# Three score banks and three filler banks in a post-norm attention layer, with fillers and PV visits placed anew

## The chip, the cores and the metric

The kernel runs on one core of a Trainium2 chip. The metric is the time of one launch in microseconds, as the device counts it; the median of several runs is given. One more execution was taken by the hardware profiler, and all rows below come from it.

## What is computed

One transformer layer with post-norm, in fp32: B = 4 sequences of S = 1024 tokens, D = 128, H = 16 heads of K = 64, and a feed-forward part with 512 hidden units whose weights are the product of butterfly stages.

```python
q, k, v = (einsum('BSE,EHK->BSHK', x, w) for w in (w_q, w_k, w_v))
logits = einsum('BSHK,BMHK->BSHM', q, k) / sqrt(64)      # causal mask added
a = einsum('BSHM,BMHK->BSHK', softmax(logits + mask), v)
x = layernorm(x + einsum('BSHK,EHK->BSE', a, w_o))
h = gelu(butterfly(x @ W_exp + b_exp, up_weights) + up_bias)
x = layernorm(x + butterfly(h, down_weights) @ W_con + b_con + down_bias)
```

## The kernel before

The attention is cut into 32 **units** (`UNITS`): one pair of heads of one sequence. A unit has 12 **steps** (`STEPS`, line 47): the queries are taken in two chunks of 512 columns, and step (qc, kt) is the tile of 128 keys kt against chunk qc. Chunk 0 has steps 0 to 3, chunk 1 steps 4 to 11. Steps 0 to 3 and 8 to 11 lie on the diagonal; there the columns are 512, 384, 256 and 128, elsewhere 512.

In each step TensorE makes the scores of both heads, two matmuls each (lines 666 and 670), ScalarE takes the exponential out of the bank (line 836), GpSimd masks the diagonal (line 478) and adds up the probabilities (lines 493 to 502), and later TensorE multiplies by V (line 691, called PV here: four matmul instructions a step, the two heads side by side in halves of the array). The scores of head h in step s use score bank (2s + h) mod `NSC`; `exp_done` guards the bank. PV of several steps is done in one **visit**. `PV_AFTER` says after which step's scores which PV steps come; negative ones are steps of the unit before (-5 is step 7, -1 is step 11).

Between all that stand **fillers**, the work for the next unit, each of which writes one of `NWORK` work banks in turn and has to wait until the filler that had the bank before is drained (`take_work`, line 573 on):
- `proj` (lines 592 to 594): q or k of the next unit for one chunk. ScalarE copies the high part (line 773), VectorE subtracts it for the low part (line 885). `proj (0, 0)` is made one unit earlier than the others.
- `v` (602 to 604): V for two tiles and two units, drained by ScalarE.
- `max` (616): scores of the next unit once more, of which VectorE takes the row maximum (lines 960, 963). `MAXES` has 21 of them.
- `mt` (621): the transposed maxima; VectorE casts them (973), and a DMA puts them into row K of QL (line 390), for which the second score matmul of the next unit waits (`m_landed`).
- `norm` (653): sums of the probabilities of the unit before, by ones, in 32-column parts of the array. ScalarE copies them out (823). Then come DMA RCOL (395), VectorE's reciprocal (1024), DMA RROW (398), two broadcasting DMAs R (401), and `scale` on VectorE (1030), which frees the PV banks O. The first PV step of each chunk waits for it (`o_free`).
- `out` (631), `lay` (624), `x1` (636), `w2` (640): output projection and preparations of the feed-forward part.

`FILL[s]` has three lists of fillers for step s: BETWEEN the scores of its two heads, BEHIND them, and LATE, behind the PV visit. Every engine walks the same order: TensorE in `window` (line 695 on), ScalarE in its loop over steps, VectorE in its own `window`. VectorE does `recip` after the fillers of step `RECIP_AFTER` and `scale` after those of `SCALE_AFTER`. GpSimd composes the butterfly weights in steps `COMPOSE_AFTER`. The PSUM banks are two for scores (SC), two for O and four WORK, eight in all.

After the last unit the feed-forward part runs on TensorE (`up`, line 741, and `down`, line 753), with four hidden banks and two y banks out of SC and WORK.

Of the kernel before, what the change touches and what calls it, by code (L numbers as in the profile page):

```python
# [72 lines left out]

PV_AFTER = {1: [-5, -4, -3, -2, -1], 8: [0, 1, 2, 3], 9: [4, 5, 6]}
PV_LEFT = [s + NS for ss in PV_AFTER.values() for s in ss if s < 0]
# [10 lines left out]
FILL = [[[], [], []] for _ in range(NS)]  # L86
FILL[0] = [[], [], [("proj", 1, 0)]]
FILL[1] = [[], [("proj", 0, 1), ("proj", 1, 1)], [("norm", 1)] + MAXES[0:1]]
FILL[2] = [[], [("v", 0)], MAXES[1:2]]
FILL[3] = [MAXES[2:3], MAXES[3:5], []]  # L90
FILL[4] = [[], [("v", 1)] + MAXES[5:6], []]
FILL[5] = [MAXES[6:7], [], MAXES[7:9]]
FILL[6] = [[], [], MAXES[9:11]]
FILL[7] = [MAXES[11:13], [], MAXES[13:14]]
FILL[8] = [MAXES[14:15], [], MAXES[15:17]]
FILL[9] = [MAXES[17:18], MAXES[18:21], []]
FILL[10] = [[("mt",)], [("proj", 0, 0)], []]
COMPOSE_AFTER = [4, 5, 9]
RECIP_AFTER = 2
SCALE_AFTER = 6  # L100
OUT_AT = ((11, 1), (11, 2))
FILLERS = [(s, place, f) for s in range(NS) for place in range(3) for f in FILL[s][place]]
# [9 lines left out]
assert all(len(ops) == 1 for ops in COMPOSE.values()) and max(unit for unit, _ in COMPOSE) < UNITS  # L112
NWORK = 4
LAY_UNITS = TILES // 2
# [51 lines left out]

NSC = 2
assert 2 * NS % NSC == 0 and LAST_PROJ in PREFETCH

# [19 lines left out]
def post_norm_layer(nc, x, w_q, w_k, w_v, w_o, W_exp, b_exp, up_w, up_b, down_w, W_con, b_con, down_b, out):  # L189
    ctx = ExitStack()  # L190
    with ctx:
# [105 lines left out]
        def lays_after(n):  # L297
# [4 lines left out]
        lay_banks = [SC[0][:, :], SC[1][:, :], O[0][:, :], O[1][:, :]]  # L302
        hid_banks = [SC[0][:, :], SC[1][:, :], WORK[(LAST_NORM - 1) % NWORK][:, :],
                     WORK[LAST_NORM % NWORK][:, :]]
        y_banks = [WORK[LAST_OUT % NWORK], WORK[(LAST_OUT + 1) % NWORK]]

# [244 lines left out]
        def _(pe):  # L551
# [182 lines left out]
            def up(g):  # L734
                pe.wait_ge(x1t_copied, g + 1)
                for t_ in range(HT):
                    if g == 0 and t_ >= 2:
                        evacuated(LAST_NORM - 3 + t_)
                    if g > 0:
                        pe.wait_ge(gelu_done, (g - 1) * HT + t_ + 1)  # L740
                    nc.tensor.matmul(hid_banks[t_], W1[:, t_ * P:(t_ + 1) * P], x1T[g % EARLY_GROUPS], start=True,  # L741
                                     stop=True).then_inc(hid_ready, 1)
# [393 lines left out]
```

## Time and profile before

| what | us |
|---|---|
| runs: median (lowest to highest) of 3 | 1051.42 (1051.22 to 1052.35) |
| the profiled execution | 1050.42 |
| its span, first to last instruction | 1048.5 |
| busy: TensorE matmuls | 1014.8 (97%) |
| busy: VectorE | 753.1 (72%) |
| busy: GpSimd | 757.2 (72%) |
| busy: ScalarE | 602.8 (57%) |
| mean granted TensorE clock | 0.989 |

The profile calls the engines PE (TensorE matmuls), PEld (its weight loads), DVE (VectorE), ACT (ScalarE), POOL (GpSimd) and SP. A matmul's time in the timeline runs from its start to its modelled end and overlaps the next one's; what it costs the sequence is seen in the distance of the starts.

### The profile page before, as it was taken

How to read it: one execution, taken by the hardware profiler on the slowest of the kernel's cores; microseconds unless marked ns; L12 is line 12 of the kernel's file. 1: busy time of each engine (PE TensorE's matmuls, PEld its weight loads, DVE VectorE, ACT ScalarE, POOL GpSimd, SP SyncE). 2: the span in 40 equal slices, each digit the busy share in tenths (PEclk: the TensorE clock that was granted, in tenths of full speed). 3: DMA queues.
4: the chain of work that ended last, by engine and by line, in shares of the span. 5: the costliest groups of instructions: out<-in, count | busy, mean ns of one | idle time of the engine just before them, and what ended most of it. 6: DMA issues, size and time to landing. Idle time of an engine off the chain costs nothing.

```text
span 1048.5 us, 17665 instructions
## 1 busy us (share of the span) xinstructions
PE 1014.8 (97%) x5816; PEld 697.7 (67%) x5816; DVE 753.1 (72%) x2013; ACT 602.8 (57%) x1214; POOL 757.2 (72%) x725
## 2 busy tenths in 40 slices
PE   4799999999999999999999999999999999999997
PEld 3556667676667766767666766676666676665576
DVE  6666777677677777776778777877777778773446
ACT  4355566665566565666666656666555655664431
POOL 6278877777779777777778877777777887777322
PEclk9699999999999999999999999999999999999999
DMA  7112223223131223232232222332313212220002
GB/s 222 44 45 67 59 58 82 63 82 79 45 81 42 73 52 83 62 82 62 64 80 55 63 58 53 82 82 63 81 43 81 68 47 72 62 62 22 22 19 63
DMA packets 45800, 68.69 MB, mean 66 GB/s; under 512 B 15079, under 2 KB 21515, under 8 KB 45710
## 3 DMA queue, kind: packets, MB, share of 16 engines
q1 hardware_dynamic: 45710, 67.57, 25.2%
q8 instruction: 47, 0.77, 0.3%
q14 instruction: 43, 0.35, 0.1%
HBM read 31.11 MB, written 2.36 MB: 32 GB/s over the span
## 4 chain that ended last, share of the span: by engine, by line
PE 91%; DMA 3%; DVE 2%; POOL 2%; issue 1%; SPq 1%; ACT 0%; POOLq 0%; DVEq 0%; ACTq 0%
PE O L691 25%; PE WORK L616 14%; PE SC L666 13%; PE SC L670 12%; PE WORK L631 5%; PE WORK L653 3%; PE WORK L753 3%; PE WORK L594 3%; PE WORK L592 3%; PE WORK L593 3%; PE WORK L602 1%; PE WORK L604 1%; PE WORK L603 1%; PE SC L741 1%; PE WORK L741 1%; DMA R<-RROW 1%
## 5 line engine op out<-in xcount | busy, mean ns | idle before, releaser
L836 ACT ACTIVATE PR<-SC 128x512 f32<-128x512 f32 (+3 forms) x768 | 354.9, 490 | 278.2 <-PE SC L670 251.9
L493 POOL TENSOR_TENSOR SUM<-SUM,PR 128x1024 f32<-128x1024 f32 (+3 forms) x256 | 418.9, 1636 | 14.9 <-POOL SUM L502 0.5
L960 DVE CUSTOM_DVE_ANT_0 WORK<-WORK,CMASK 128x128 f32<-128x128 f32 (+3 forms) x512 | 239.1, 513 | 65.9 <-PE WORK L616 65.8
L666 PE MATMUL SC<-QH,KHL 128*128 128x512 f32 (+3 forms) x768 | 271.9, 359 | 4.8 <-ACT PR L836 3.2
L670 PE MATMUL SC<-QL,KH 128*128 128x512 f32 (+3 forms) x768 | 262.8, 346 | 0.0
L478 POOL TENSOR_SCALAR_AFFINE_SELECT PR<-PR 128x256 f32<-128x256 f32 x256 | 105.8, 415 | 206.1 <-ACT PR L836 205.9
L616 PE MATMUL WORK<-KHL,QH 128*128 128x512 f32 (+3 forms) x768 | 225.1, 361 | 5.4 <-DMA KH<-KHL 4.0
L691 PE MATMUL O<-PR,VLO 128*64 128x512 f32 (+3 forms) x1024 | 200.0, 522 | 1.2 <-DVE OT L1030 1.0
L666 PEld LDWEIGHTS SC<-QH,KHL 128*128 128x128 f32 x768 | 145.2, 189 | 63.8 <-ACT PR L836 29.2
L616 PEld LDWEIGHTS WORK<-KHL,QH 128*128 128x128 f32 x768 | 135.8, 191 | 56.0 <-issue 35.3
L963 DVE TENSOR_REDUCE MP<-WORK 128x1 f32<-128x512 f32 x256 | 164.2, 683 | 4.7
L670 PEld LDWEIGHTS SC<-QL,KH 128*128 128x128 f32 x768 | 145.5, 189 | 10.3
L885 DVE TENSOR_TENSOR QL<-WORK,QH 64x512 fp32r<-64x512 f32 x128 | 88.0, 688 | 78.8 <-ACT QH L773 77.6
L502 POOL TENSOR_TENSOR SUM<-PR 128x768 f32<-128x768 f32 x64 | 136.6, 2134 | 1.4 <-ACT PR L836 1.4
L691 PEld LDWEIGHTS O<-PR,VLO 128*64 128x64 f32 x1024 | 64.9, 136 | 105.6 <-issue 77.6
L885 DVE TENSOR_TENSOR KHL<-WORK,KHL 64x512 fp32r<-64x512 f32 x128 | 88.1, 689 | 38.3 <-ACT KHL L773 36.2
L773 ACT ACTIVATE QH<-WORK 64x512 fp32r<-64x512 f32 x128 | 75.6, 590 | 27.8 <-PE WORK L594 27.0
L773 ACT ACTIVATE KHL<-WORK 64x512 fp32r<-64x512 f32 x128 | 75.8, 593 | 4.7 <-PE WORK L594 1.4
L691 PE MATMUL O<-PR,VHI 128*64 128x256 f32 (+3 forms) x512 | 74.3, 432 | 0.0
L960 DVE DVE_READ_ACCUMULATOR2_ANT MP<- 128x1 f32 x512 | 72.1, 141 | 0.0
L691 PEld LDWEIGHTS O<-PR,VHI 128*64 128x64 f32 x512 | 36.8, 137 | 52.6 <-issue 46.0
L631 PE MATMUL WORK<-WOT,OT 128*128 128x128 f32 x512 | 63.7, 278 | 0.0
(100 smaller groups left out, 1070.5 us busy)
## 6 DMA issues: line engine op xcount, KB each, us to landing
QH<-QH SPq DMA_DIRECT2D x128, 128.0 KB, 2.3
KH<-KHL SPq DMA_DIRECT2D x128, 128.0 KB, 2.3
R<-RROW SPq DMA_DIRECT2D x64, 256.0 KB, 3.9
SW<-in_L_ffn_up_weights_dram SPq DMA_DIRECT2D x9, 512.0 KB, 4.6
SW<-_L_ffn_down_weights_dram SPq DMA_DIRECT2D x9, 512.0 KB, 4.4
out_dram<-X SPq DMA_DIRECT2D x8, 256.0 KB, 2.3
X<-in_L_attn_x_BSE_dram SPq DMA_DIRECT2D x1, 512.0 KB, 4.6
WQKV<-in_L_attn_w_q_dram SPq DMA_DIRECT2D x1, 512.0 KB, 5.4
```

The lines of the kernel that those rows point to most:

```text
L493: nc.gpsimd.tensor_tensor(total, total, prob(unit, s), ALU.add).then_inc(add_done, 1)
L502: nc.gpsimd.tensor_tensor(total, first[:, :, START[s]:], prob(unit, s), ALU.add).then_inc(add_done, 1)
L616: t = nc.tensor.matmul(w[:, at_col:at_col + n], QH[:, nxt, h, qt * P:(qt + 1) * P], KHL[:, nxt, h, lo:lo + n], start=True, stop=True)
L631: t = nc.tensor.matmul(w[:, k * P:(k + 1) * P], attended(pair, qc)[:, k * P:(k + 1) * P], WOT[:, pair % PAIRS, :], start=pair < last, stop ...
L666: nc.tensor.matmul(dst, KHL[:, par, h, kt * P:(kt + 1) * P], QH[:, par, h, q0:q0 + n], start=True, stop=False)
L670: nc.tensor.matmul(dst, KH1[:, par, h, kt * P:(kt + 1) * P], QL[:, par, h, q0:q0 + n], start=False, stop=True).then_inc(scores_ready, 1)
L691: t = nc.tensor.matmul(O[qc][h * K:(h + 1) * K, START[s]:], values(unit, kt)[:, h * K:(h + 1) * K], p[:, h, :], start=kt == 0, stop=s == L ...
L773: return nc.scalar.activation(dst, src, ACT.Copy)
L836: nc.scalar.activation(prob(unit, s)[:, h, :], SC[use % NSC][:, 0:n], ACT.Exp, scale=K ** -0.5).then_inc(exp_done, 1)
L885: return nc.vector.tensor_tensor(dst, src, hi_part.bitcast(F32), ALU.subtract)
L960: op = nc.vector.tensor_tensor_reduce(cols, cols, CMASK[:, CH - n:], 1.0, LOWEST, ALU.add, ALU.max, cell)
L963: op = nc.vector.tensor_reduce(cell, cols, AX_X, ALU.max)
```

## The change

The score banks become three, the work banks three; with the two O banks it is eight as before. The PV visits stand after steps 0, 2, 8 and 10 in place of 1, 8 and 9. The fillers are placed anew: three projections together in step 0, norm in step 2 ahead of the PV visit there, both v fillers in step 3, `mt` and `proj (0, 0)` behind the visit of step 10, and one of the output fillers with them. `scale` comes one step later, a compose step stands in step 0 in place of 4. The hidden banks of the feed-forward part are the three score banks and one work bank.

```diff
-PV_AFTER = {1: [-5, -4, -3, -2, -1], 8: [0, 1, 2, 3], 9: [4, 5, 6]}
+PV_AFTER = {0: [-5, -4, -3], 2: [-2, -1], 8: [0, 1, 2, 3], 10: [4, 5, 6]}
...
-FILL[0] = [[], [], [("proj", 1, 0)]]
-FILL[1] = [[], [("proj", 0, 1), ("proj", 1, 1)], [("norm", 1)] + MAXES[0:1]]
-FILL[2] = [[], [("v", 0)], MAXES[1:2]]
-FILL[3] = [MAXES[2:3], MAXES[3:5], []]
-FILL[4] = [[], [("v", 1)] + MAXES[5:6], []]
-FILL[5] = [MAXES[6:7], [], MAXES[7:9]]
-FILL[6] = [[], [], MAXES[9:11]]
-FILL[7] = [MAXES[11:13], [], MAXES[13:14]]
-FILL[8] = [MAXES[14:15], [], MAXES[15:17]]
-FILL[9] = [MAXES[17:18], MAXES[18:21], []]
-FILL[10] = [[("mt",)], [("proj", 0, 0)], []]
-COMPOSE_AFTER = [4, 5, 9]
+FILL[0] = [[("proj", 1, 0), ("proj", 0, 1), ("proj", 1, 1)], [], []]
+FILL[1] = [MAXES[0:1], MAXES[1:2], MAXES[2:3]]
+FILL[2] = [[], [("norm", 1)], MAXES[3:5]]
+FILL[3] = [[("v", 0), ("v", 1)] + MAXES[5:6], [], MAXES[6:7]]
+FILL[4] = [[], MAXES[7:8], []]
+FILL[5] = [[], [], MAXES[8:9]]
+FILL[6] = [MAXES[9:10], [], MAXES[10:11]]
+FILL[7] = [MAXES[11:12], [], MAXES[12:13]]
+FILL[8] = [MAXES[13:14], MAXES[14:16], MAXES[16:18]]
+FILL[9] = [[], MAXES[18:19], MAXES[19:20]]
+FILL[10] = [MAXES[20:21], [], [("mt",), ("proj", 0, 0)]]
+COMPOSE_AFTER = [0, 5, 9]
 RECIP_AFTER = 2
-SCALE_AFTER = 6
-OUT_AT = ((11, 1), (11, 2))
+SCALE_AFTER = 7
+OUT_AT = ((10, 2), (11, 1))
...
-NWORK = 4
+NWORK = 3
...
-NSC = 2
+NSC = 3
...
-        hid_banks = [SC[0][:, :], SC[1][:, :], WORK[(LAST_NORM - 1) % NWORK][:, :],
-                     WORK[LAST_NORM % NWORK][:, :]]
+        hid_banks = [SC[0][:, :], SC[1][:, :], SC[2][:, :], WORK[LAST_NORM % NWORK][:, :]]
...
-                    if g == 0 and t_ >= 2:
-                        evacuated(LAST_NORM - 3 + t_)
+                    if g == 0 and t_ == NSC:
+                        evacuated(LAST_NORM)
```

## Rows read from the trace of the kernel before

**Rows 1.** The page: engine busy time; the granted clock in 40 slices, in tenths

```profile
PE 1014.8 (97%) x5816; PEld 697.7 (67%) x5816; DVE 753.1 (72%) x2013; ACT 602.8 (57%) x1214; POOL 757.2 (72%) x725
PEclk9699999999999999999999999999999999999999
```

**Rows 2.** TensorE's waits at score banks (us, times, longest): 79 to 920 us; whole span

```profile
PE SC L666 <- ACT PR L836: 1.2, 1, 1.2
...
PE SC L666 <- ACT PR L836: 3.2, 6, 1.2
```

**Rows 3.** Timeline of TensorE, 506 to 519 us (start, us, engine, line)

```profile
506.90 0.27 PE L621 MATMUL WORK<-IDN,NEGM 128*128 128x128 f32 x1
...
510.40 0.39 PE L670 MATMUL SC<-QL,KH 128*128 128x512 f32 x1
...
511.56 0.40 PE L594 MATMUL WORK<-XTL,WST 128*128 128x512 f32 x1
...
513.64 0.39 PE L594 MATMUL WORK<-XTL,WST 128*128 128x512 f32 x1
513.96 1.08 PE L691 MATMUL O<-PR,VLO 128*64 128x512 f32 x4
...
517.12 1.06 PE L653 MATMUL WORK<-SUM,ONES 128*32 128x512 f32 x8
518.12 0.50 PE L616 MATMUL WORK<-KHL,QH 128*128 128x128 f32 x2
```

**Rows 4.** Timeline of TensorE, 524 to 537 us

```profile
524.86 0.42 PE L666 MATMUL SC<-QH,KHL 128*128 128x512 f32 x1
525.12 0.39 PE L670 MATMUL SC<-QL,KH 128*128 128x512 f32 x1
...
528.50 2.37 PE L691 MATMUL O<-PR,VLO 128*64 128x512 f32 x16
...
533.20 2.79 PE L691 MATMUL O<-PR,VLO 128*64 128x512 f32 x12
535.93 0.38 PE L666 MATMUL SC<-QH,KHL 128*128 128x256 f32 x1
536.15 0.28 PE L670 MATMUL SC<-QL,KH 128*128 128x256 f32 x1
```

**Rows 5.** Timeline of TensorE's weight loads, 513 to 515 us

```profile
513.19 0.19 PEld L593 LDWEIGHTS WORK<-XTH,WST 128*128 128x128 f32 x1
513.42 0.19 PEld L594 LDWEIGHTS WORK<-XTL,WST 128*128 128x128 f32 x1
513.96 0.20 PEld L691 LDWEIGHTS O<-PR,VLO 128*64 128x64 f32 x4 [0.35 <-ACT PR L836]
514.44 0.14 PEld L691 LDWEIGHTS O<-PR,VHI 128*64 128x64 f32 x2 [0.29 <-issue]
514.87 0.14 PEld L691 LDWEIGHTS O<-PR,VHI 128*64 128x64 f32 x2 [0.28 <-issue]
```

**Rows 6.** Score matmuls of 512 columns by form: busy us, mean ns, idle before

```profile
L666 PE MATMUL SC<-QH,KHL 128*128 128x512 f32 x384 | 158.8, 413 | 4.5 <-ACT PR L836 3.0 <-issue 1.5
...
L670 PE MATMUL SC<-QL,KH 128*128 128x512 f32 x384 | 151.4, 394 | 0.0
```

**Rows 7.** Timeline of ScalarE: one projection's two copies

```profile
511.99 1.20 ACT L773 ACTIVATE KHL<-WORK 64x512 fp32r<-64x512 f32 x2
```

**Rows 8.** Timeline of VectorE: one projection's subtractions; scale

```profile
515.19 1.39 DVE L885 TENSOR_TENSOR QL<-WORK,QH 64x512 fp32r<-64x512 f32 x2 [0.58 <-ACT QH L773]
...
527.54 1.29 DVE L1030 TENSOR_TENSOR OT<-O,R 128x512 f32<-128x512 f32 x2 [0.47 <-DMA R<-RROW]
```

**Rows 9.** VectorE's waits for R, whole span (us, times, longest)

```profile
DVE OT L1030 <- DMA R<-RROW: 15.2, 17, 6.0
```

**Rows 10.** Timeline of SyncE's DMA queue: issue of the row of maxima

```profile
507.51 0.55 SPq L390 DMA_DIRECT2D QL<-NROW  x1
```

**Rows 11.** DMA issues, 506 to 512 us: KB each, median us to landing

```profile
QL<-NROW SPq DMA_DIRECT2D x1, 8.0 KB, 1.8
```

## The prediction

> **What bounds the kernel now.** I read the page's engine shares first, then TensorE's waits, then its timeline, then the engines that feed it. The page has TensorE at 1014.8 of 1048.5 us, and the granted clock at nine tenths or more of 2.4 GHz in all but the second of 40 slices [rows 1]. A busy TensorE may still lose time inside matmuls that start late, so the share alone decides nothing. Two further views do. In the 841 us of the loop between the first and the last units, TensorE waits once for anything, 1.2 us at a score bank [rows 2]. And in the timeline its matmuls start one behind the other: a matmul of 512 columns takes 0.23 us from its start to the next one's (the loads for L593 and L594 in [rows 5] are 0.23 apart). So TensorE's own sequence sets the time, and an edit is worth what it adds to or takes from that sequence, plus any wait it makes or removes.
>
> What is in the sequence beyond the columns? The PV matmuls use the array in halves (128*64, two heads beside each other), everything else in the loop but norm uses all of it. The timeline in [rows 3] shows the way in: L594 at 513.64 would be followed at 513.87, but the first L691 starts at 513.96, **0.09 us late**. The weight loads in [rows 5] show why: within a run of one kind the weights are loaded ahead (those of the L594 that starts at 513.64 at 513.42), while the first PV weights load only at 513.96, with the matmul itself. Inside the run the loads come 0.43 us apart for a pair of heads, but the first pair takes 0.48 (513.96 to 514.44): **0.05 more**. The way out: the visit at 533.20 has six pairs, 6 x 0.43 = 2.58, plus the 0.05, and the next matmul would start at 535.83; it starts at 535.93, **0.10 late**, and the 256-column matmul behind it takes 0.22 instead of 0.12, **0.10 more** [rows 4]. One separate visit therefore costs 0.09 + 0.05 + 0.10 + 0.10 = **0.34 us** besides its work, by what shows at its ends, whatever it holds: the visit and norm from 513.96 to 518.12 come, with ten pairs and norm's two sets of four, to 3.01 + 0.86 of columns in 4.16, which leaves 0.29 for the inside of two modes [rows 3].
>
> **The change part by part.** *PV visits.* Before there are three blocks a unit: after step 1 (five PV steps, norm right behind them), after 8, after 9. After the change there are four: after 0 (three steps), after 2 (two steps, norm right ahead of them), after 8, after 10. The columns are the same; one block more is new. The previous unit's two visits stand in units 1 to 31: 31 x 0.34 = **+10.5 us**, all on TensorE's sequence, so all on the path. Norm in front of PV in place of behind costs nothing more: the block goes into one mode, over to the other and out of it either way, and norm keeps its 1.00 us (517.12 to 518.12) [rows 3].
>
> The Trainium skill, TensorEngine Tiling (Array Packing), section Key Properties, says that a change of tiling mode drains TensorE. This trace agrees with the drain and gives it the price of 0.34 us for in and out. By that rule the change as a whole is bought with one more drain a unit; it is the rule that speaks against it.
>
> *Third score bank.* What can it give? Score matmuls of line 666 (the ones that wait for a bank) average 413 ns at 512 columns, those of 670, which never do, 394: 19 ns x 384 = 7.3 us is the most that can hide there [rows 6]; part of it is the way out of other modes. In a unit's timeline the late starts at score banks are of the kind of 524.86 to 525.12, 0.26 in place of 0.23 [rows 4], at two or three places of the unit: nearer to 0.055 x 31 = 1.7 us. I take **-1.7** and keep -7.3 as the bound. It does more where few fillers stand between scores, in the first two units and the last: over the whole span the visible waits for a score bank are 3.2 us in 6 places [rows 2]. In the last unit the visit after step 8 waits for R behind them, so not all comes back; I take **-2.0** for all edges, between 0 and -4.
>
> *Three filler banks.* A filler waits for the drain of the third before it, not the fourth. The tight place is the start of the unit: three projections stand together in step 0. Reckoned from its first score: two score matmuls 0.47, the first projection's third matmul at 0.94, and ScalarE starts 0.43 us after such a start (511.99 against 511.56), so at 1.37 [rows 3, 7]. ScalarE needs 1.20 for each projection [rows 7]: the first is handed on at 2.57. VectorE needs 1.39 each and a little between them [rows 8], three in a row: 6.8. TensorE comes to the filler that needs the third projection's bank after 0.47 + 2.08 (projections) + 0.47 + 0.09 + 2.51 (PV) + 0.10 + 0.35 + 0.23 + 0.35 + 0.23 = 6.88 (narrower ones by columns from the 0.23 of 512; PV of 1408 columns as two times two pairs of 0.43 and two of 0.32, and 0.15 of the mode). Spare 0.1, which the semaphores nearly take. Norm comes at 7.63. The others, gone through in the same way, have 0.15 us or more. I take 31 x 0.02 = **+0.7**, from 0 to 31 x 0.5 = +15 if VectorE comes late by half a microsecond (see the third rival). The prologue has 29 fillers through three banks, with VectorE as its bound and a DMA wait that absorbs part: **+0.5**, 0 to +1.5.
>
> *Norm later, and the chain behind it.* Norm stands one step later. Behind it: the evacuation, RCOL, recip, RROW, the broadcast R, then scale, whose first half frees O for PV after step 8. In the unit shown scale starts at 527.54, 10.42 us after norm (517.12), and its two halves take 1.29, so the first ends at 11.06 [rows 3, 8]. VectorE waits for R 17 times, 15.2 us in all and 6.0 the longest [rows 9]: some 0.6 us at a time in half of the units, 0.47 in the one shown. So the end moves by about half a microsecond to either side of 11. TensorE reaches the visit 11.38 us after norm today (528.50 minus 517.12) [rows 3, 4]; in the new order the work between is 1.00 norm, 0.80 + 0.10 PV, 0.41 two maxes, 0.44 step 3, 1.43 v, 0.23 + 0.22 maxes, 4 x 0.94 steps 4 to 7 with 0.94 of maxes, step 8 with 0.64, and 0.09 in: 11.2. So only the late units wait, some 0.05 us on average: **+1.5**, 0 to +12.
>
> *mt behind the visit of step 10, proj (0,0) behind it.* mt (506.90) to the second score matmul of the next unit (510.40) is 3.50 us today [rows 3]; in the new order 0.11 + 0.70 + 1.76 + 0.45 + 0.31 = 3.3. What the matmul waits for: the cast and issue at 507.51, 0.61 after mt, plus 1.8 of transfer = 2.4 [rows 10, 11]. No wait in units with an output filler; 0. The moved maxes and compose steps (GpSimd, at 72% busy, is no nearer to the path) and the new bank list of the tail change no sum on TensorE: 0.
>
> Sum: 10.5 - 1.7 - 2.0 + 0.7 + 0.5 + 1.5 = **+9.5 us**. The profiled execution took 1050.42 us (span 1048.5, 1.9 around it); with the sum 1059.9. The median is 1.0 above the profiled one: **1060.9 us**, +0.9%.
>
> **The rivals.** *The new block is hidden or as cheap as nothing* (the change of mode costs only where something else waits too): 1051.4 - 3.7 + 2.7 = **1050.4**, no change. Against it: three visits of different size show the same cost, at places where all inputs had long been there.
>
> *Faster: the score bank hides more than the visit costs.* Place: the score matmuls of steps 4 to 8, where the plan after the change has one or two fillers a step. If all 7.3 us are bank waits and the new visit costs less than 0.14 us, it ends below 1049: 31 x 0.1 - 7.3 - 2.0 + 2.7 = -3.5, **1048**. From 0.14 us a visit on it isn't faster. The measured 0.34 speaks against.
>
> *Bank starvation.* The 0.05 us of the third projection's bank is missed by VectorE, e.g. behind an output sum or a normalise step of the step before: each 0.5 us is 15: **1076**. For it: the spare is nil. Against: VectorE has waits of its own for ScalarE ahead of the first projection.
>
> *The R chain ends last* at the visit after step 8: each 0.35 us more there is +11: **1072**. For it: 0.1 us of spare against a spread of about 1 us.
>
> **How the numbers follow.** Forecast 0.66, block hidden 0.08, faster 0.08, starvation 0.10, R chain 0.08. The forecast's own bounds are 1056 to 1066. Leaving 0.1 out on either side, the range goes to 1053 below (part of the block hidden) and to 1070 above (either wait in part). About 0.2% is what a measurement of this kernel can tell from no change: faster 0.08, same 0.08, slower 0.84.
>
> **What would show it.** Right: TensorE still over 96% busy; visits at steps 0 and 2 each with a late first start (0.09) and a late matmul behind (0.10 + 0.10); a unit some 0.35 us longer; no wait lines for work banks. Starvation would show in TensorE's waits for VectorE's L885 or L960 at line 616 in step 1; the chain as waits of L691 for L1030; a faster kernel as a unit that is not longer though it has four blocks. What would make it wrong: a mode change whose cost depends on its neighbours, or a wait inside today's 'busy' matmuls that I took for the cost of a mode.

## Result: slower by 2.2%, and the profile after

| | before | after |
|---|---|---|
| median of the runs beside each other, us | 1051.87 (4 runs) | 1075.35 (4 runs, 1072.56 to 1077.79) |
| ratio to before, 95% interval | 1 | 1.0223 [1.0197, 1.0249] |
| profiled execution, us | 1050.42 | 1072.56 |
| its span, us | 1048.5 | 1070.6 |
| mean granted clock | 0.989 | 0.988 |

The change costs 23.5 us. The forecast had 9.5 and the range ended at 1070. In the lines quoted from here on, the line numbers of the kernel after are one lower than those of before: the filler that waits at L616 before waits at L615, the scores' L666 and L670 are L665 and L669, PV's L691 is L690, VectorE's L885, L960, L985, L1013 and L1030 are L884, L959, L984, L1012 and L1029, and so on. The kernels with four filler banks keep the numbers of before.

The profile's page of the kernel after: the engines' busy time with its share of the span, and the shares of the chain that ended last. They answer [rows 1]; the line of the granted clock is the same as there. The third line is the chain of the kernel before.

```profile
PE 1028.8 (96%) x5816; PEld 710.6 (66%) x5816; DVE 778.5 (73%) x2013; ACT 611.0 (57%) x1214; POOL 763.4 (71%) x725
PE 82%; DVE 9%; DMA 5%; issue 1%; ACT 1%; POOL 1%; SPq 1%; POOLq 0%; ACTq 0%; DVEq 0%
PE 91%; DMA 3%; DVE 2%; POOL 2%; issue 1%; SPq 1%; ACT 0%; POOLq 0%; DVEq 0%; ACTq 0%
```

TensorE is busy for 1028.8 us in place of 1014.8, with exactly as many matmuls and the same clock; its idle time went from 33.7 to 41.8 us. So 14.0 of the 22.1 us sit inside what the page calls busy, and 8.1 outside. The chain that ended last runs over VectorE for 9% of the span (before: 2%). That is the first sign that not only TensorE's own sequence got longer.

TensorE's waits in the loop, from 79 to 940 us (engine, what it made, line, the engine and line waited for: us in all, how many, the longest). They answer [rows 2], where one wait of 1.2 us stood for the whole loop:

```profile
PE O L690 <- DVE OT L1029: 3.3, 3, 1.4
PE WORK L591 <- DVE X L984: 3.2, 8, 0.6
PE WORK L615 <- DVE KHL L884: 1.7, 4, 0.5
PE SC L669 <- DMA QL<-NROW: 1.1, 2, 0.8
PE WORK L620 <- DVE NEGM L966: 0.9, 1, 0.9
```

With one more of 0.2 these are 10.4 us, and nearly all are waits for VectorE: a PV visit for the scale of O, a projection for the output sum, a max filler for a projection's cast, mt for the last maxes. A view of waits lists only idle time; a matmul that starts late while its forerunner still counts as busy is not in it. So I went through the timeline by distances from start to start. It shows this in the loop: the third projection (of the three that stand together in step 0) late in nine of the units by 0.48 to 0.81 (some 5 us, and 1 us behind it), the maxes of step 1 late by up to 0.70 in six units, and what stands behind the third of them late by 0.1 in some twenty (some 4.5), PV behind step 8 late by 0.96, 1.46 and 1.13 in the first unit of the second, third and fourth sequence (3.5), the row of maxima that the DMA puts into QL late in three of the first four units after unit 0 (2.4), and mt late twice (1.7). Each is measured against the usual distance at its place, so together they need not give the whole.

One such unit on TensorE (start, duration, engine, line, operation, output and inputs, shape, count, and in brackets the idle time ahead with its releaser); it answers [rows 3]:

```profile
579.91 0.39 PE L593 MATMUL WORK<-XTL,WST 128*128 128x512 f32 x1
580.61 0.50 PE L591 MATMUL WORK<-XTH,WST 128*128 128x512 f32 x1 [0.31 <-DVE X L984]
...
586.20 0.45 PE L615 MATMUL WORK<-KHL,QH 128*128 128x384 f32 x1 [0.29 <-DVE KHL L884]
```

And VectorE in the same stretch:

```profile
578.91 0.93 DVE L1012 TENSOR_SCALAR X<-X,MV,RSTD 128x128 f32<-128x128 f32 x1
579.87 0.69 DVE L984 TENSOR_TENSOR X<-WORK,X 128x512 f32<-128x512 f32 x1
...
581.91 1.39 DVE L884 TENSOR_TENSOR KHL<-WORK,KHL 64x512 fp32r<-64x512 f32 x2
...
584.75 1.39 DVE L884 TENSOR_TENSOR KHL<-WORK,KHL 64x512 fp32r<-64x512 f32 x2
586.18 0.30 DVE L959 CUSTOM_DVE_ANT_0 WORK<-WORK,CMASK 128x128 f32<-128x128 f32 x1
```

The third projection (580.61) should start 0.23 us after 579.91, that is at 580.14. Its bank is the one of the output filler, which stands three fillers before it. VectorE frees it with the output sum at 579.87 to 580.56, and that had stood behind a normalise step (578.91) that took 0.93 us: 0.47 us late. The three casts of projections then go back to back until 586.14, and the max at 586.20 has to wait for the last. With four banks, as before, neither waits.

Which units are late follows from VectorE's list. An output sum stands at the start of every unit from unit 3 on. In every second one from unit 12 to unit 30 a normalise stands ahead of it, and nine of these ten are the ones with the late third projection (in the tenth, unit 22, the normalise took 0.36 us). Four statistics of 0.87 us in all and their aggregates, between the sum and the first cast, stand in units 9, 10, 17, 18, 25 and 26. These are the units whose maxes are latest (0.70 in 17 and 25, 0.45 in 18 and 26, 0.37 in 9), but for unit 10 with 0.09.

### The profile page after: what moved, and what is told of

Same layout as the page of the kernel before. It is cut to its first block, busy times and chain, and to the rows that moved or that the text cites. A ratio compares the mean times of both kernels' runs of the same rounds, so it can differ in the third digit from the quotient of the medians.

```text
span 1070.6 us, 17665 instructions
## 1 busy us (share of the span) xinstructions
PE 1028.8 (96%) x5816; PEld 710.6 (66%) x5816; DVE 778.5 (73%) x2013; ACT 611.0 (57%) x1214; POOL 763.4 (71%) x725
## 3 DMA queue, kind: packets, MB, share of 16 engines
HBM read 31.11 MB, written 2.36 MB: 31 GB/s over the span
## 4 chain that ended last, share of the span: by engine, by line
PE 82%; DVE 9%; DMA 5%; issue 1%; ACT 1%; POOL 1%; SPq 1%; POOLq 0%; ACTq 0%; DVEq 0%
PE O L690 23%; PE WORK L615 13%; PE SC L665 11%; PE SC L669 11%; PE WORK L630 3%; PE WORK L652 3%; PE WORK L752 3%; PE WORK L591 2%; DVE QL L884 2%; PE WORK L593 2%; PE WORK L592 2%; PE SC L740 2%; DMA R<-RROW 1%; DVE X L1012 1%; PE WORK L601 1%
## 5 line engine op out<-in xcount | busy, mean ns | idle before, releaser
L492 POOL TENSOR_TENSOR SUM<-SUM,PR 128x1024 f32<-128x1024 f32 (+3 forms) x256 | 419.2, 1638 | 14.6 <-ACT PR L835 0.5
L959 DVE CUSTOM_DVE_ANT_0 WORK<-WORK,CMASK 128x128 f32<-128x128 f32 (+3 forms) x512 | 243.0, 511 | 74.7 <-PE WORK L615 72.0
L477 POOL TENSOR_SCALAR_AFFINE_SELECT PR<-PR 128x256 f32<-128x256 f32 x256 | 108.7, 425 | 222.1 <-ACT PR L835 220.8
L665 PE MATMUL SC<-QH,KHL 128*128 128x512 f32 (+3 forms) x768 | 265.5, 351 | 1.5 <-issue 1.5
L669 PE MATMUL SC<-QL,KH 128*128 128x512 f32 (+3 forms) x768 | 261.8, 345 | 1.9 <-DMA QL<-NROW 1.9
L615 PE MATMUL WORK<-KHL,QH 128*128 128x512 f32 (+3 forms) x768 | 238.6, 363 | 6.2 <-DVE KHL L884 3.3
L690 PE MATMUL O<-PR,VLO 128*64 128x512 f32 (+3 forms) x1024 | 201.6, 526 | 7.0 <-DVE OT L1029 7.0
L962 DVE TENSOR_REDUCE MP<-WORK 128x1 f32<-128x512 f32 x256 | 172.2, 687 | 19.1 <-PE WORK L615 19.1
L665 PEld LDWEIGHTS SC<-QH,KHL 128*128 128x128 f32 x768 | 145.2, 189 | 36.8 <-issue 14.9
L615 PEld LDWEIGHTS WORK<-KHL,QH 128*128 128x128 f32 x768 | 135.8, 190 | 36.9 <-issue 12.3
L669 PEld LDWEIGHTS SC<-QL,KH 128*128 128x128 f32 x768 | 145.2, 189 | 20.2 <-DMA QL<-NROW 2.8
L690 PEld LDWEIGHTS O<-PR,VLO 128*64 128x64 f32 x1024 | 65.5, 137 | 104.4 <-issue 73.8
L884 DVE TENSOR_TENSOR QL<-WORK,QH 64x512 fp32r<-64x512 f32 x128 | 88.0, 688 | 56.5 <-ACT QH L772 54.6
L884 DVE TENSOR_TENSOR KHL<-WORK,KHL 64x512 fp32r<-64x512 f32 x128 | 88.2, 689 | 23.5 <-ACT KHL L772 21.4
L690 PE MATMUL O<-PR,VHI 128*64 128x256 f32 (+3 forms) x512 | 81.2, 439 | 0.0
L690 PEld LDWEIGHTS O<-PR,VHI 128*64 128x64 f32 x512 | 34.0, 136 | 66.8 <-issue 40.3
L959 DVE DVE_READ_ACCUMULATOR2_ANT MP<- 128x1 f32 x512 | 72.1, 141 | 0.0
```

Of the source, the lines that this page charges most:

```text
L477: nc.gpsimd.affine_select(out=tri, in_=tri, compare_op=ALU.is_ge, fill=fill, base=0, pattern=[[0, 2], [1, P]], channel_multiplier=-1).then ...
L492: nc.gpsimd.tensor_tensor(total, total, prob(unit, s), ALU.add).then_inc(add_done, 1)
L615: t = nc.tensor.matmul(w[:, at_col:at_col + n], QH[:, nxt, h, qt * P:(qt + 1) * P], KHL[:, nxt, h, lo:lo + n], start=True, stop=True)
L665: nc.tensor.matmul(dst, KHL[:, par, h, kt * P:(kt + 1) * P], QH[:, par, h, q0:q0 + n], start=True, stop=False)
L669: nc.tensor.matmul(dst, KH1[:, par, h, kt * P:(kt + 1) * P], QL[:, par, h, q0:q0 + n], start=False, stop=True).then_inc(scores_ready, 1)
L690: t = nc.tensor.matmul(O[qc][h * K:(h + 1) * K, START[s]:], values(unit, kt)[:, h * K:(h + 1) * K], p[:, h, :], start=kt == 0, stop=s == L ...
```

## Experiments

All kernels compute the whole layer; only plans and bank counts differ. Times are medians with the range and the number of runs, ratios stand against the kernel before on the same chip (1051.6 to 1051.9). Distances of norm are those of two neighbouring units for which the view of waits lists nothing. The first five take the change apart, the others take its waits apart.

### One block more, on the plan before

```diff
-PV_AFTER = {1: [-5, -4, -3, -2, -1], 8: [0, 1, 2, 3], 9: [4, 5, 6]}
+PV_AFTER = {1: [-5, -4, -3], 2: [-2, -1], 8: [0, 1, 2, 3], 9: [4, 5, 6]}
```

> The kernel before with one edit: PV steps 10 and 11 of the unit before are multiplied after step 2 in place of step 1 (31 more visits). Theory A (a mode change costs 0.34 us wherever it stands): +10.5 us over before, 1062. Theory B (the loss of the change is in one more visit alone): +22 to +24, 1075. Theory C (all of the loss comes from the filler banks, a visit costs nothing of its own): 1051 to 1053.

Measured: 1066.51 us (1064.52 to 1067.57, 4), ratio 1.0137 [1.0122, 1.0152]: +14.6. Norm's start in two neighbouring units, of before and then of this kernel:

```profile
253.82 1.07 PE L653 MATMUL WORK<-SUM,ONES 128*32 128x512 f32 x8
282.97 1.06 PE L653 MATMUL WORK<-SUM,ONES 128*32 128x512 f32 x8
```

```profile
256.58 1.06 PE L653 MATMUL WORK<-SUM,ONES 128*32 128x512 f32 x8
286.08 1.06 PE L653 MATMUL WORK<-SUM,ONES 128*32 128x512 f32 x8
```

29.15 and 29.50 us: the block costs 0.35, 31 of them 10.9. The whole came out 4.5 above the 1062 that I had expected. Beyond the blocks, the profiled execution shows some 3.5 us in the loop, mostly late starts of maxes (up to 0.36) in every second unit, and a last unit with tail that is 2.6 longer. So the block's price is as forecast, and this plan has so little slack that a shift of two PV steps makes some maxes late even with four filler banks.

### The banks alone, on the plan before

```diff
-NWORK = 4
+NWORK = 3
-NSC = 2
+NSC = 3
```

(and the tail's list of banks as in the change)

> The kernel before with three score banks and three filler banks and nothing else replanned. Theory A: the score banks give back up to 2 us; the filler banks cost what VectorE is late by, in the old plan perhaps 0 to 5 us: 1050 to 1056. Theory C (three filler banks starve TensorE in any plan): +15 or more, 1066 and up. Theory D (the third score bank alone is worth something): below 1049.

Measured: 1124.71 us (1123.88 to 1128.28), ratio 1.0704 [1.0683, 1.0725]: **+73**, the largest loss but one of all. I had expected next to nothing of it. TensorE's waits from 79 to 940 us, a late max on TensorE, and VectorE beside it:

```profile
PE WORK L615 <- DVE MP L959: 21.6, 27, 2.2
```

```profile
534.85 0.40 PE L669 MATMUL SC<-QL,KH 128*128 128x512 f32 x1
...
535.87 0.50 PE L615 MATMUL WORK<-KHL,QH 128*128 128x512 f32 x1 [0.63 <-DVE MP L959]
```

```profile
534.14 1.28 DVE L1029 TENSOR_TENSOR OT<-O,R 128x512 f32<-128x512 f32 x2
```

VectorE works its list in order. While it scales O for 1.28 us, it frees no filler bank, and the plan before has its maxes in tight groups around that place. Four banks bridge it, three don't. The list of waits holds only 21.6 of the 73 us; but the order of TensorE's matmuls is that of before, so the starts can be compared one by one: in the loop the maxes start 52 us later in sum, the scores behind them 11. A third score bank gives nothing visible back here. So the change bears three filler banks only because it also regroups the fillers.

### The new plan on the old banks, and on two score banks with three fillers

```diff
-NWORK = 3
+NWORK = 4
-NSC = 3
+NSC = 2
```

> The changed kernel with two score banks and four filler banks as before: the new plan alone. Theory A: the waits for VectorE at filler banks (third projection 6 us, maxes 5 us) go, but with few fillers between the scores of steps 4 to 7 two score banks don't do: a bank comes back 1.42 us after its scores started, and the plan has 1.17 us a step there, 0.25 us in three steps of each unit, 24 us: 1080 to 1090. Rival (the score banks were idle anyway): 1062 to 1065.

Measured: 1100.85 us (1100.28 to 1101.57), ratio 1.0465 [1.0449, 1.048]: 25.5 slower than the kernel after, and 11 above what I had expected at most. The second kernel keeps NWORK at 3 and takes one score bank away (`NSC = 2`).

> The changed kernel with two score banks in the attention, three filler banks (the third score bank is used in the feed-forward part alone): what the third score bank is worth in the new plan. Theory A: +15 to +25 over the changed kernel, 1090 to 1100. Rival (as the forecast had it for the old plan, up to 2 us): 1075 to 1078.

Measured: 1111.53 us (1108.96 to 1111.83), ratio 1.0558 [1.054, 1.0575]: 36 slower than the kernel after, again 11 above the expectation. TensorE in the first of these two kernels, from one start of two score steps and one filler to the next such start, and ScalarE beside it:

```profile
517.17 0.50 PE L666 MATMUL SC<-QH,KHL 128*128 128x512 f32 x1
...
518.21 0.40 PE L616 MATMUL WORK<-KHL,QH 128*128 128x512 f32 x1
518.59 0.50 PE L666 MATMUL SC<-QH,KHL 128*128 128x512 f32 x1
```

```profile
516.51 1.09 ACT L836 ACTIVATE PR<-SC 128x512 f32<-128x512 f32 x2 [0.38 <-PE SC L670]
517.94 1.09 ACT L836 ACTIVATE PR<-SC 128x512 f32<-128x512 f32 x2 [0.34 <-PE SC L670]
```

Between the two starts TensorE has five matmuls of 512 columns, 5 x 0.23 = 1.15 us, and takes 1.42 for them. That is a bank's own round: ScalarE's two exponentials take 1.09, and then it has to wait 0.34 until TensorE has filled the banks again, while TensorE has waited for ScalarE. The plan of the change runs steps this close together and holds its fillers in bulk elsewhere; there the third score bank is worth 36 us. The plan before seldom meets that round (one listed wait at a score bank in the loop, [rows 2]). So the bank and the plan belong together in both directions: new banks on the old plan +73, new plan on the old banks +49, both together +23.5.

These two kernels have the same plan and the same two score banks in the attention, so they also price the fourth filler bank on the new plan: 1111.53 - 1100.85 = **10.7 us**. TensorE's waits at filler banks from 79 to 940 us, first with four filler banks, then with three (the waits for mt left out of the second list are the same 1.4):

```profile
PE WORK L621 <- DVE NEGM L967: 1.4, 2, 0.7
```

```profile
PE WORK L591 <- DVE X L984: 3.2, 9, 0.6
PE WORK L615 <- DVE KHL L884: 0.9, 4, 0.3
```

With four banks there is no wait of a projection for the output sum and none of a max for a cast; with three both are there. By starts, projections are 6.3 us later in the loop and maxes 2.0. The waits for mt are there with four banks too.

### Two visits in place of three, on the plan before

```diff
-PV_AFTER = {1: [-5, -4, -3, -2, -1], 8: [0, 1, 2, 3], 9: [4, 5, 6]}
+PV_AFTER = {1: [-5, -4, -3, -2, -1], 8: [0, 1, 2, 3, 4, 5, 6]}
```

> The kernel before with PV steps 4 to 6 moved from the visit after step 9 into the one after step 8: one block of PV less in each of 32 units. Theory A (a mode change costs 0.34 to 0.36 us wherever it stands, VectorE has slack in the old plan with four filler banks): 32 x 0.35 = 11 us less, 1041. Rival (VectorE is so near to the bound that 5 us of TensorE without a max leave it idle, and the maxes behind it wait): 1048 to 1056.

Measured: 1126.19 us (1124.27 to 1127.08), ratio 1.0703 [1.0687, 1.0719]. A block less and yet +74, where I had expected -11. Its waits:

```profile
PE WORK L621 <- DVE NEGM L967: 63.7, 32, 2.3
```

The visit behind step 9 was cover: while TensorE does PV there, VectorE ends the last maxes that mt needs. Without it TensorE waits some 2 us for them in each of the 32 units. A visit can't be taken away for 0.34 us if it hides somebody; this is what made me look for a pair of visits whose joining hides nobody.

### The normalise step moved to step 5

The rival of the starvation named a normalise step or an output sum ahead of the projections' casts. This kernel takes the normalise away from there.

```diff
-NORMALISE_AT = {t: ((t // TILES + 1) * PAIRS + 3 + t % TILES, 10) ...
-NORMALISE_AT |= {t: ((B - 1) * PAIRS + 3 + t % TILES // 2, 9 + t % 2) ...
+NORMALISE_AT = {t: ((t // TILES + 1) * PAIRS + 3 + t % TILES, 5) ...
+NORMALISE_AT |= {t: ((B - 1) * PAIRS + 3 + t % TILES // 2, 5 + t % 2) ...
```

> The changed kernel, with each normalise step of VectorE moved from step 10 (9 and 10 in the last sequence) to step 5 (5 and 6). Theory A: the 10 waits of the third projection for the output sum (0.5 to 0.8 us each, 6 us with what follows them) go, and a part of the waits at the third and fourth max: 1066 to 1070. Theory B (only the visit counts): 1075 as it is.

Measured: 1080.40 us (1078.55 to 1081.59), ratio 1.027 [1.0255, 1.0285]: 5 slower, not 7 faster. The third projection's waits are gone, so the normalise was their cause; but the maxes behind its new place wait:

```profile
PE WORK L615 <- DVE MP L962: 5.4, 6, 1.3
```

In steps 5 and 6 the gap between fillers is too short for the step, which takes 0.48 to 2.36 us there. A miss of the number, and a hint that the step is dearer than the 0.35 us of its best case.

### The same, to step 9

```diff
-NORMALISE_AT = {t: ((t // TILES + 1) * PAIRS + 3 + t % TILES, 10) ...
+NORMALISE_AT = {t: ((t // TILES + 1) * PAIRS + 3 + t % TILES, 9) ...
```

> The changed kernel with the normalise step of VectorE one step earlier (9 in place of 10) for the first two sequences: into the place before mt where VectorE stands idle 1.6 us a unit in the changed kernel. Theory A (the third projection waits for the bank of the output sum because normalise stands ahead of it): seven or eight of the ten waits there go, 4 to 5 us less and nothing new in their place: 1070 to 1071. Rival (as when it was moved to step 5, any place behind which VectorE has maxes to do costs more than it saves): 1076 or more.

Measured: 1075.95 us (1074.21 to 1076.78), ratio 1.0226 [1.0212, 1.024]: no change to the kernel after, where I had expected 5 us less. Waits of TensorE over the whole span:

```profile
PE WORK L620 <- DVE NEGM L966: 9.0, 12, 1.4
```

Most of the third projection's waits went, mt's came in their place, and PV waited in five units of the loop in place of three. A short normalise of this kernel, and what GpSimd did beside it:

```profile
392.14 0.35 DVE L1012 TENSOR_SCALAR X<-X,MV,RSTD 128x128 f32<-128x128 f32 x1
```

```profile
391.99 0.42 POOL L477 TENSOR_SCALAR_AFFINE_SELECT PR<-PR 128x256 f32<-128x256 f32 x1
```

### The normalise in the gap behind mt's cast

Before the next unit's first projection, VectorE waits for TensorE and ScalarE. If the normalise is issued right behind the cast of mt, it stands in that wait and ahead of nobody that has its input. The edit puts the loop over NORMALISE_AT behind the consumer of mt, and skips step 10 at its old place (the last unit excepted):

```diff
                             consume(u, f, n)
+                        if f[0] == "mt":
+                            for t, when in NORMALISE_AT.items():
+                                if when == (u, s):
+                                    dve.wait_ge(rstd_made, t // TILES + 1)
+                                    normalise_tile(t, x1_made)
```

> The changed kernel with the same placing of normalise, nothing else. Theory A: the waits of the third projection in the eight units behind a normalise step go (4.6 us) without the waits for scale and at mt that came when it stood at step 9: 1070 to 1071. Rival (the VectorE work only moves): 1075.

Measured: 1068.22 us (1067.46 to 1068.77), ratio 1.0157 [1.0143, 1.0171]: **7.1 us** less than the kernel after, by nothing but the place of the normalise steps in VectorE's list. It fell 2 us below what I had expected. The order of TensorE's matmuls is the same in both, so the starts can be compared: in the loop the projections give back 5.6 us and the maxes 2.2, which the expectation had left out, while other starts come 2.8 later.

### One block less on the new plan, three times

Norm and both of the previous unit's visits go into one block behind step 0:

```diff
-PV_AFTER = {0: [-5, -4, -3], 2: [-2, -1], 8: [0, 1, 2, 3], 10: [4, 5, 6]}
+PV_AFTER = {0: [-5, -4, -3, -2, -1], 8: [0, 1, 2, 3], 10: [4, 5, 6]}
-FILL[0] = [[("proj", 1, 0), ("proj", 0, 1), ("proj", 1, 1)], [], []]
+FILL[0] = [[("proj", 1, 0), ("proj", 0, 1), ("proj", 1, 1)], [], [("norm", 1)]]
-FILL[2] = [[], [("norm", 1)], MAXES[3:5]]
+FILL[2] = [[], [], MAXES[3:5]]
```

> The changed kernel, with all five PV steps of the unit before after step 0 and norm right behind them, so three blocks a unit as before. Theory A: 31 x 0.34 = 10.5 us less, and the waits for scale after step 8 (3.5 us) and at the third max (3.4 us) go, since norm comes 1 us earlier and the maxes 1.7 us later: 1057 to 1062. Theory C (filler banks are all): 1070 to 1075.

Measured: 1077.28 us (1075.73 to 1078.08), ratio 1.024 [1.0225, 1.0255]; a miss by 15 to 20. The block's 0.34 us is saved, and each unit waits at a max bank, 0.36 us on average in the list and up to 0.5:

```profile
PE WORK L615 <- DVE MP L959: 11.3, 31, 0.5
```

The visit and norm in step 2 were the cover behind which VectorE caught up with the maxes. The next kernel draws the five maxes of steps 2 to 4 apart on top of it:

```diff
-FILL[2] = [[], [], MAXES[3:5]]
-FILL[3] = [[("v", 0), ("v", 1)] + MAXES[5:6], [], MAXES[6:7]]
-FILL[4] = [[], MAXES[7:8], []]
+FILL[2] = [[], [], MAXES[3:4]]
+FILL[3] = [[("v", 0), ("v", 1)] + MAXES[4:5], [], MAXES[5:6]]
+FILL[4] = [[], MAXES[6:7], MAXES[7:8]]
```

> The changed kernel with all five PV steps and norm after step 0, and the fifth to ninth max each one place later, so that VectorE has time: Theory A (in the run without that, the 0.34 us of the visit came back and went into a wait of 0.5 us for the bank of the second max before, in every unit): 15 us less than that run, 1062. Rival (VectorE's backlog from the three projections is only moved to the next place): 1070 to 1077.

Measured: 1069.61 us (1068.01 to 1070.73), ratio 1.0166 [1.0151, 1.0181], so 7.7 less, half of the 15 that I had expected; the rest of the wait moved on to v:

```profile
PE WORK L601 <- DVE MP L959: 5.5, 30, 0.3
```

A v filler is drained by another engine than the maxes. So the third of these kernels puts v 0 among them, where it gives VectorE time, and the normalise to step 9:

```diff
+FILL[2] = [[], [], [("v", 0)]]
+FILL[3] = [MAXES[3:4], [("v", 1)], MAXES[4:5]]
+FILL[4] = [MAXES[5:6], MAXES[6:7], MAXES[7:8]]
```

> One block for PV and norm after step 0, the first v filler (which ScalarE drains) moved between the maxes in step 2, the other fillers of steps 3 and 4 spread, normalise in step 9. Theory A (what the change loses is one block of PV a unit and the waits for VectorE, and both can be taken out of it): the 0.34 us a unit wait of the run before goes (10 us) and most waits of the third projection (5 us): 1069.6 - 15 = 1055. Rival (VectorE's backlog appears elsewhere): 1062 or more. Below 1049 would mean that three score banks pay after all.

Measured: 1056.58 us (1055.37 to 1059.02, 5), ratio 1.0049 [1.0037, 1.0062]: as expected. What waits is left in it:

```profile
PE WORK L620 <- DVE NEGM L966: 6.7, 9, 1.4
```

### The block back in, while mt waits

The last kernel with the visit split again (`0: [-5, -4, -3], 2: [-2, -1]`), norm staying in the first block.

> The same with the last two PV steps of the unit before after step 2, so one block of PV more in each of 31 units: the price of a block in the plan with three filler banks. Theory A: +0.36 us x 31 = +11 over the run beside it. Rival (in the new plan a block gives VectorE time, so that part of it is got back): +3 to +7.

Measured: 1075.89 us (1074.56 to 1076.53), ratio 1.023 [1.0214, 1.0245]: 19.3 more, not 11. The undisturbed units are 0.32 longer, which is 10 us; the other 9 are mostly these, 15.2 in place of 6.7:

```profile
PE WORK L620 <- DVE NEGM L966: 15.2, 21, 1.4
```

With the normalise in step 9, mt waits for the last maxes in 21 units in place of 9. Why in more of them was not tried; but I could not use this pair to price the block, hence the next two.

### The cleaned pair: nearly all waits taken away, with and without the block

The kernel with one block and v 0 among the maxes, with the normalise behind mt's cast:

> The one-block plan with v early (1056.6), with the normalise step of VectorE between mt's cast and the next projection, where VectorE waits 1.65 us for ScalarE in every unit, in place of ahead of the last maxes. Theory A (TensorE's waits for the maxima at mt, 0.75 us in six units of the first three sequences, are the 1.1 us of normalise): 6 x 0.75 = 4.5 less, 1052, and perhaps a little under the kernel before. Rival (it isn't normalise, the maxes are late anyway): 1056 to 1057.

Measured: **1050.07 us** (1048.66 to 1052.74, 11 runs) against 1051.69 (15 runs), ratio 0.9984 [0.9974, 0.9993]. It is the best of all kernels here. It is 0.16% below the one before, and the interval ends only just below 1. What TensorE waits for from 79 to 930 us:

```profile
PE SC L669 <- DMA QL<-NROW: 1.3, 2, 0.8
PE WORK L620 <- DVE NEGM L966: 0.7, 1, 0.7
```

Its twin has the visit split again and nothing else changed:

> The first of these three with the last two PV steps after step 2 again: the price of one more block where normalise is out of the way. Theory A (a block costs 0.34 us of mode change and pushes the last maxes nearer to mt only behind normalise): +10 to +12 over the first, 1063. Rival (a block costs what the earlier pair of runs showed, 19 us, because any later place of the maxes makes mt wait): +17 to +20, 1070.

Measured: 1061.13 us (1060.17 to 1061.37), ratio 1.0089 [1.0075, 1.0102]: 11.06 more, as expected, 0.357 for each of 31 blocks. Norm's starts in two neighbouring units, first of the one-block kernel, then of its twin:

```profile
251.09 1.07 PE L652 MATMUL WORK<-SUM,ONES 128*32 128x512 f32 x8
280.06 1.06 PE L652 MATMUL WORK<-SUM,ONES 128*32 128x512 f32 x8
```

```profile
252.08 1.06 PE L652 MATMUL WORK<-SUM,ONES 128*32 128x512 f32 x8
281.38 1.06 PE L652 MATMUL WORK<-SUM,ONES 128*32 128x512 f32 x8
```

28.97 and 29.30. The 0.33 in an undisturbed unit and the 0.357 from the whole kernel enclose the 0.34 that was read off the ends of the visits before. The latter still has some waits in it: by starts, mt is late by 3.1 us in four units of the twin, by 1.5 in two of the one-block kernel.

### The ladder

| kernel | us | step |
|---|---|---|
| after | 1075.35 | |
| normalise behind mt's cast | 1068.22 | -7.1 |
| and norm in the first block, v 0 among the maxes, maxes drawn apart | 1061.13 | -7.1 |
| and one block less | 1050.07 | -11.1 |
| before | 1051.7 | +1.6 |

Of the 23.5 us (23.7 with the 1051.7 of this table), 11.1 are the block, 14.2 went by placing the same work otherwise, and -1.6 is the sum of all that is left. The 14.2 are not all waits at filler banks. The second step was tried as a whole only, but the traces show what is in it: before it PV still started 4.3 us late in four units and behind it in none, and an undisturbed unit went from 29.41 to 29.30. PV no longer waits since norm stands earlier: TensorE then reaches the visit after step 8 behind norm by 13.1 us in place of 11.07. The kernels of the section before show that drawing the maxes apart was worth 7.7 in the absence of the block.

The -1.6 is a sum of larger terms, too. In the profiled executions an undisturbed unit of the best kernel is 0.18 us shorter than before (28.97 against 29.15) and unit 0 is 2.7 shorter. Against it stand a last unit with tail that is 3.35 longer, and 4.1 us of late starts: 2.6 at the row of maxima in units 1, 2 and 4, and 1.5 at mt in units 28 and 30.

## Why the prediction was right or wrong

**What bounds it:** right for the kernel before, and half of the truth for the change. "TensorE's own sequence sets the time" holds only while VectorE frees banks ahead of it, and how far ahead it was I had not read.

**One block more, +10.5:** right. Two neighbouring norms of the kernel after stand 29.41 apart, against 29.15 before:

```profile
255.10 1.07 PE L652 MATMUL WORK<-SUM,ONES 128*32 128x512 f32 x8
284.51 1.06 PE L652 MATMUL WORK<-SUM,ONES 128*32 128x512 f32 x8
```

That is +0.26 in a unit without a listed wait, where the sum had 0.34 - 0.055 = 0.285. About 0.1 of it is such a late start behind the third max, though. The cleaned pair gives the block alone: 0.33, and 11.1 for the whole. The Trainium skill, TensorEngine Tiling (Array Packing), section Key Properties, says that a change of tiling mode drains TensorE; the runs agree, with 0.35, 0.33 and 0.32 us a unit for one block more in three pairs of kernels, hidden in none. The rival "block hidden" falls by the same numbers.

**Third score bank, -1.7:** that it is near the -1.6 which remains is luck, since the latter is a sum of other terms (see the ladder); an undisturbed unit gave 0.18 where the sum had 0.055, for the bank and the new order together. The reasoning about its worth was incomplete. It was read as the waits that the plan before has at score banks. Its worth to the plan after is 36 us, because that plan has places where two banks would make 1.42 us of 1.15. The waits of a kernel tell what a resource is worth to its present order, not to the new one.

**Three filler banks, +0.7: this is the step that failed**, at "Spare 0.1" and "The others, gone through in the same way, have 0.15 us or more". It is the term of the sum that was mis-sized. It measured some 10.5 us by the late starts of the kernel after (6 at the third projections, 4.5 at the maxes), and 10.7 us between the two kernels with two score banks. Three things were wrong in it. First, the walk went through one unit, [rows 3, 8], and looked at the casts alone, with VectorE's list beginning empty. The third projection itself needs the bank of the output filler. VectorE frees that 1.36 us after the start of a unit when nothing stands ahead, 0.57 us before it is due; in every second unit from unit 12 on a normalise stands ahead, and in nine of them the third projection starts 0.48 to 0.81 us late. Second, it took each step of VectorE at one duration; the normalise takes 0.35 to 2.25 us. Third, "0.15 us or more" is no margin when durations move by more than that. Even the 0.1 was not there: in an undisturbed unit VectorE ends the third cast at 283.61, and the max that needs its bank starts at 283.66 with its weights loaded only then, which costs 0.1. The tight place was rightly found, and so was the mechanism, but with 10% for it in place of most of the chance. The words "VectorE has waits of its own for ScalarE ahead of the first projection" were what kept it low. They hold even in a late unit (0.30 us ahead of the cast at 518.74), but that wait stands behind the output sum and does nothing for it.

**R chain, +1.5, 0 to +12:** held, with another pattern than forecast. The terms listed for TensorE's way from norm to the visit add up to 11.0, not 11.2, and it measured 11.07; scale's first half ended 10.66 to 11.00 behind norm in 27 of the 30 units after unit 0 and before the last. So not "only the late units wait, some 0.05 us on average": three PV visits wait, 0.96 to 1.46 us, all in the first unit of a sequence, 3.5 us in all. VectorE was not busy there; it stood idle ahead of scale and waited for R:

```profile
528.26 0.32 SPq L397 DMA_DIRECT2D RROW<-RCOL  x1
531.38 1.12 SPq L400 DMA_DIRECT2D R<-RROW  x2
```

```profile
536.14 1.29 DVE L1029 TENSOR_TENSOR OT<-O,R 128x512 f32<-128x512 f32 x2 [1.67 <-DMA R<-RROW]
```

Recip and the issue of RROW came at their usual time, but R could be issued only 3.12 us behind RROW, when that had landed; in the other units it is 1.45. The same holds in units 8 and 24. Why this small transfer took twice as long there is open. VectorE's own waits for R over the whole span became fewer, 11.3 us in six places in place of 15.2 in 17 [rows 9], since scale now comes a step later:

```profile
DVE OT L1029 <- DMA R<-RROW: 11.3, 6, 6.2
```

**mt, 0:** missed by some 4 us. The row of maxima was late in units 1, 2 and 4, 2.4 us; the first two follow units without an output filler, the third does not, so "No wait in units with an output filler" held but for once. And mt waited 0.94 and 0.75 us in units 28 and 30, for the last maxes; that it waits for them as well as the score matmul for its transfer was not looked at. Neither belongs to the filler banks: the best kernel has 4.1 us of the same, and with four filler banks on the new plan mt is late too, by 3.0 us.

**Edges, -2.0:** held in part. Unit 0 is 2.0 us shorter (27.72 against 29.74), but the last unit with the tail is 1.8 longer (102.06 against 100.26), so they cancel. The prologue, forecast at +0.5, was 0.3 shorter: unit 0 starts at 42.15 in place of 42.44.

**The signs that were named:** a late first start and late followers at the visits, yes; TensorE over 96% busy, just; "no wait lines for work banks", no. "TensorE's waits for VectorE's L885 or L960 at line 616 in step 1" is precisely what stands in the waits of after as L615 <- L884, with more lines of the same kind around it.

**The starvation rival's number**, 1076, is near to the measured 1075.35, but by another division: it had no block in it beyond the forecast's and reckoned half a microsecond in every unit at one place. What happened is some 6 us there and the rest of the waits at other places. That its total fits is partly chance.

## What to carry to other kernels

A bank taken from a pool is priced by the consumer's worst stretch, not by a typical unit: go through every kind of unit (here those with a normalise or with statistics at their start), lay the whole list of the draining engine against the bank's due time, and give each of its steps the longest duration in the trace. Here the margins that failed were 0.1 and 0.57 us. Where such waits show, look first whether a short step of that engine can stand in a gap that it has anyway: moving the normalise steps won 7 us, and only with norm and the maxes moved as well did the price of the block read cleanly.

## What the runs showed of the hardware that was not expected

**A VectorE step whose time depends on GpSimd.** The normalise, 128x128 from and to SBUF, takes 0.35 us in the quiet and up to 2.25. What goes with it is an add of GpSimd under way. VectorE in the kernel after, and GpSimd in the same stretch:

```profile
397.83 1.26 DVE L1012 TENSOR_SCALAR X<-X,MV,RSTD 128x128 f32<-128x128 f32 x1
```

```profile
397.71 2.16 POOL L492 TENSOR_TENSOR SUM<-SUM,PR 128x512 f32<-128x512 f32 x2
```

and in the best kernel:

```profile
417.82 1.97 DVE L1012 TENSOR_SCALAR X<-X,MV,RSTD 128x128 f32<-128x128 f32 x1
```

```profile
417.90 1.81 POOL L492 TENSOR_TENSOR SUM<-SUM,PR 128x768 f32<-128x768 f32 x1
```

The second one ends at 419.79, 0.08 us behind the end of the add at 419.71, and so it goes in 22 of the 24 cases in the loop of the kernel after (in two of these it took no longer for that). GpSimd's affine_select can't be judged from these traces: the normalise that began at 392.14 took only its 0.35, but it too ended 0.08 us behind the affine_select (391.99 and 0.42), and that is when its own 0.35 were over, too. And not every step of GpSimd holds it. In the tail of the kernel after, the last of these four normalises began at 1034.89, behind the start of a GpSimd step of 1.04 us, and took 0.34:

```profile
1034.15 1.08 DVE L1012 TENSOR_SCALAR X<-X,MV,RSTD 128x128 f32<-128x128 f32 x4
```

```profile
1034.84 1.04 POOL L525 TENSOR_TENSOR RSTD<-RSTD,HALF 128x4 f32<-128x4 f32 x1
```

The Trainium skill, SBUF — State Buffer, section Who interferes with whom, says that VectorE and GpSimd share a port pair under an exclusive lock, and names VectorE's tensor_scalar, in its fast modes, among the steps that can contend for it. The adds agree with it; whether the step ran in that mode, no row shows, and the last case doesn't fit it as it stands (though the spans that the profile gives for GpSimd are rough). No kernel here took the adds away, so the lock is read from the order of the ends, not tried. In the best kernel the same 1.97 us costs nothing, since it stands where VectorE would wait.

**A stall costs more than itself.** Behind a listed wait of TensorE the waiting matmul takes 0.50 us in place of 0.39 (580.61 above), and the next one starts 0.34 behind it in place of 0.23. Its weights were loaded only with it:

```profile
580.61 0.19 PEld L591 LDWEIGHTS WORK<-XTH,WST 128*128 128x128 f32 x1 [0.75 <-DVE X L984]
```

So 0.11 us comes on top of the wait; the same 0.11 stands behind each of the nine late third projections.
